# Router logits as one accumulated product in 16 columns, both halves of attention together, and a recurrence step moved into an expert product

## The chip, the cores and the metric

The kernel runs on 1 core of one Trainium2 chip. The time is that of one execution on the device in microseconds (us), the median of several runs. TensorE (PE) multiplies, VectorE (DVE), ScalarE (ACT) and GpSimd (POOL) do the elementwise work, SyncE (SP) issues most transfers. PEld is TensorE's loading of weights, which can run beside its matmuls.

## The reference, cut to what matters

```
x = x + attn_a(layernorm(x))         # gated linear attention, then a GELU feed-forward inside
x = x + ffn(layernorm(x))            # mixture of experts
x = x + attn_b(layernorm(x))         # recurrence h = tanh(x_t B + h A^T), then C and W_out
x = x + ffn(layernorm(x))            # the same mixture of experts again

def ffn(x):                          # per token, 8 experts, 2 chosen
    logits = x @ router_w.T          # (tokens, 8)
    probs = softmax(logits)
    topk_vals, topk_idx = top_k(probs, 2)
    topk_w = topk_vals / (topk_vals.sum(-1) + 1e-6)
    out = ((x @ expert[topk_idx] + probs[topk_idx]) * topk_w).sum(over the two)
```

x has 8 batches of 1024 tokens of 256 values, all float32. The recurrence goes over the 1024 positions of a batch, one after another.

## The kernel before

The 1024 positions are cut into 32 rounds of 32 positions; with 8 batches a round has 256 tokens (`TOK`), held as 2 tiles (`TILES`) of 128 tokens. A round passes through 8 stages (the `live(it, n)` of each engine's `body`), and the stages of 8 different rounds are interleaved in one iteration of the loop: stage 1 and 2 are the linear attention, 3 its output and the feed-forward, 4 the first router and its experts (`m1`), 5 the 32 steps of the recurrence, 6 its end and the second router (`m2`), 7 the second experts. The first 8 iterations and the last 7 are written out, 24 run as a loop. All stages that this document speaks of (attention of stage 2, first experts of stage 4, the recurrence of stage 5, the second router of stage 6) run together in iterations 6 to 33, which are 28; each stage runs 32 times.

Each engine has its own order of instructions, written out by hand in its `body`, and waits on semaphores by count. There is no scheduler.

Products in full precision are made in three single-pass float32r matmuls for each chunk of 128 (`product`, L1247 to L1255: lead x lead, lead x rest, rest x lead). The left operand of each is split in a lead (`yT[:, 0]`, a copy by ScalarE) and a rest (`yT[:, 1]`, a subtraction by VectorE). An expert product (`moe`, out of `we` and `yT`) has six such matmuls of 512 columns for a pair of experts and a tile of tokens; there are 8 (`G1_0` to `G1_7`) for each router.

The recurrence has one small matmul for each step (`step`, L1271, 8 columns). ScalarE makes two tanh of it (`state_of`, L566 and L567), VectorE the split into parts that are exact in float32r (`split_state`, L858), and only then can TensorE issue the next step. The hand-written orders put one or more other products between two steps.

The router: TensorE transposes the normalised tokens (L1260), ScalarE and VectorE split them (`yT`), and `logits` (L1285) makes four float32 matmuls with `rw`, 32 stationary columns of which 8 hold the router's weights: one for each part and chunk, each in its own strip of 32 columns of the array and so in its own 32 output partitions. ScalarE copies the result into `m.y[:, 0]` (L696 for the first router, L734 for the second), `logits_by_token` (L1292) transposes it back in two 128x128 transposes, and VectorE adds the four pieces (`top_two`, L898) and picks the two experts.

Attention: `attend(i, ...)` (L1331) makes 16 matmuls for tile i, in strips of 32 columns. `attend(0)` stood ahead of step 14, `attend(1)` behind step 14 and the second router's logits. ScalarE squares the result (`osq`, L731) once both are done.

Of the kernel before, what the change touches and what calls it, by code (L numbers as in the profile page):

```python
# [39 lines left out]
ROUTED = 32  # L40
# [56 lines left out]
def build(nc, x, wts, out):  # L97
    ctx = ExitStack()
    with ctx:
# [35 lines left out]
        rw = sb("rw", [P, KC, ROUTED])  # L135
# [98 lines left out]
        late_sync = [(raw(W_1, KC * FF), wts["W1"]), (rw[:, :, 0:E], wts["router_w"]), (b1[:], wts["b1"])]  # L234
# [147 lines left out]
        def _(pool):  # L382
# [6 lines left out]
            g.memset(rw[:], 0.0)  # L389
# [143 lines left out]
        def _(act):  # L533
# [13 lines left out]
            def split_late():  # L547
                act.wait_ge(sem("weights_psum"), 2)
                act.wait_ge(sem("a_loaded"), A_LOADED)
                act.wait_ge(sem("late"), LATE)  # L550
                a.activation(a_lead, a_raw, ACT.Copy)
                a.activation(cw[ROW_LEAD:ROW_LEAD + 1, :], bout[ROW_LEAD:ROW_LEAD + 1, :], ACT.Copy)
                a.activation(bout_lead, bout[ROW_REST:ROW_REST + 1, :], ACT.Copy)
                a.activation(cw_lead, ps[0:NB, BANK["RB"], 0:D], ACT.Copy).then_inc(sem("weights_lead"), 1)
                act.wait_ge(sem("weights_rest"), REST["scaled_out"])
                a.activation(wa[:, 0, W_O:W_END], raw(W_O, W_END - W_O), ACT.Copy).then_inc(sem("weights_lead"), 1)
# [63 lines left out]
            def body(it):  # L620
# [73 lines left out]
                if live(it, 5):  # L694
                    act.wait_ge(sem("LT1"), c5)
                    a.activation(m1.y[:, 0, :], ps[:, BANK["L1"], 0:TOK], ACT.Copy).then_inc(sem("lT1"), 1)  # L696
# [35 lines left out]
                if live(it, 7):  # L732
                    act.wait_ge(sem("LT2"), c7)
                    a.activation(m2.y[:, 0, :], ps[:, BANK["L2"], 0:TOK], ACT.Copy).then_inc(sem("lT2"), 1)  # L734
# [88 lines left out]
        def _(dve):  # L823
# [15 lines left out]
            def split_late():  # L839
                dve.wait_ge(sem("weights_lead"), LEAD["late"])  # L840
                v.tensor_tensor(wa[:, 1, W_O:W_END], raw(W_O, W_END - W_O), wa[:, 0, W_O:W_END].bitcast(F32), ALU.subtract).then_inc(sem("weights_rest"), 1)
# [53 lines left out]
            def top_two(m, bank, count):  # L895

                pieces = ps[:, bank, TOK:2 * TOK].rearrange("p (i s w) -> p i s w", i=TILES, w=ROUTED)[:, :, :, 0:E]
                v.tensor_reduce(m.lg, pieces.rearrange("p i s e -> p i e s"), AX.X, ALU.add).then_inc(sem(f"lg{m.s}"), 1)  # L898
                target = value(dve, count)
                dve.wait_ge(sem("pads_zero"), 1)  # L900
                dve.wait_ge(sem(f"lg{m.s}"), target)
                for i in range(TILES):
                    ins = v.max(m.mx[:, i, :], m.lg[:, i, :])
                ins.then_inc(sem(f"mx{m.s}"), 1)
# [326 lines left out]
        def _(pe):  # L1231
# [15 lines left out]
            def product(dst, left, right, chunks):  # L1247


                n = 0  # L1250
                for c in range(chunks):
                    for lp, rp in ((0, 0), (0, 1), (1, 0)):
                        n += 1
                        ins = t.matmul(dst, left(lp, c), right(rp, c), start=(n == 1), stop=(n == 3 * chunks))  # L1254
                return ins  # L1255
# [7 lines left out]
            def moe(m, k, bank):  # L1263

                i, pr = k // PAIRS, k % PAIRS
                right = lambda p, c: we[:, p, c * E * D + pr * 2 * D:c * E * D + (pr + 1) * 2 * D]
                return product(ps[:, bank, :], lambda p, c: m.yT[:, p, c, i * P:(i + 1) * P], right, KC)
# [12 lines left out]
            def logits(m, bank):  # L1280

                for part in range(2):
                    for c in range(KC):
                        g = part * KC + c
                        ins = t.matmul(ps[ROUTED * g:ROUTED * (g + 1), bank, 0:TOK], rw[:, c, :], m.yT[:, part, c, :].bitcast(F32),  # L1285
                                       start=True, stop=True, skip_group_check=True)
                return ins

            def logits_by_token(m, bank):

                for i in range(TILES):
                    ins = t.transpose(ps[:, bank, TOK + i * P:TOK + (i + 1) * P], m.y[:, 0, i * P:(i + 1) * P], ident)  # L1292
                return ins
# [42 lines left out]
            def body(it):  # L1336
# [201 lines left out]
                if live(it, 4):  # L1538
# [6 lines left out]
                    pe.wait_ge(sem("lT1"), c4)  # L1545
# [26 lines left out]
                if live(it, 2):  # L1572
# [3 lines left out]
                    attend(0, isinstance(it, int) and it == 2)  # L1576
                if live(it, 5):
                    step(14, c5)
# [5 lines left out]
                if live(it, 2):  # L1584
                    attend(1, False).then_inc(sem("O11"), 1)
                if live(it, 5):
                    step(15, c5)
                if live(it, 4):
                    for name, count in readers(it, "G1_4"):
                        pe.wait_ge(sem(name), count)  # L1590
                    moe(m1, 4, BANK["G1_4"]).then_inc(sem("moe1"), 1)
                if live(it, 5):
                    step(16, c5)
                if live(it, 6):
                    pe.wait_ge(sem("lT2"), c6)
                    logits_by_token(m2, BANK["L2"]).then_inc(sem("L2"), 1)
# [76 lines left out]
```

## Time and profile before

| | before |
|---|---|
| runs | 1694.19 us median of 3 (1693.38 to 1694.59) |
| span of the profiled execution | 1692.7 us |
| time of the profiled execution beside its span | none given apart from the span |
| PE busy | 1591.6 us (94%) |
| PEld busy | 1324.5 us (78%) |
| DVE busy | 1274.3 us (75%) |
| ACT busy | 1051.2 us (62%) |
| POOL busy | 823.1 us (49%) |
| mean granted TensorE clock | 0.974 |

The span is from the first to the last instruction of one execution. Busy is the time in which an engine has at least one instruction in work; matmuls are pipelined and overlap, so the distance between the starts of two instructions says more than how long one is. The granted clock is 1.00 in the stretches used below, which is 2.4 GHz.

### The profile page before, as it was taken

How to read it: one execution, taken by the hardware profiler on the slowest of the kernel's cores; microseconds unless marked ns; L12 is line 12 of the kernel's file. 1: busy time of each engine (PE TensorE's matmuls, PEld its weight loads, DVE VectorE, ACT ScalarE, POOL GpSimd, SP SyncE). 2: the span in 40 equal slices, each digit the busy share in tenths (PEclk: the TensorE clock that was granted, in tenths of full speed). 3: DMA queues.
4: the chain of work that ended last, by engine and by line, in shares of the span. 5: the costliest groups of instructions: out<-in, count | busy, mean ns of one | idle time of the engine just before them, and what ended most of it. 6: DMA issues, size and time to landing. Idle time of an engine off the chain costs nothing.

```text
span 1692.7 us, 51627 instructions
## 1 busy us (share of the span) xinstructions
PE 1591.6 (94%) x16840; PEld 1324.5 (78%) x16840; DVE 1274.3 (75%) x4556; ACT 1051.2 (62%) x3851; POOL 823.1 (49%) x1294
## 2 busy tenths in 40 slices
PE   4588999999999999999999999999999999998866
PEld 3477888888888888888888888888888888887654
DVE  4566777887788778787888787887888877876544
ACT  4656666666766666666666666666666667655431
POOL 3554454554555455545454554454545545543211
PEclk7799999999999999999999999999999999999978
DMA  5211111111111111011111111111111111110000
GB/s 151 84 57 45 52 58 58 42 39 43 43 56 56 56 51 43 31 52 47 56 56 56 46 42 35 50 50 56 56 56 43 37 44 44 52 52 8 7 7 13
DMA packets 117250, 81.49 MB, mean 48 GB/s; under 512 B 42016, under 2 KB 108224, under 8 KB 117056
## 3 DMA queue, kind: packets, MB, share of 16 engines
q1 hardware_dynamic: 116208, 80.10, 15.4%
q8 instruction: 38, 0.62, 0.2%
q10 hardware_dynamic: 976, 0.54, 0.1%
q14 instruction: 28, 0.23, 0.0%
HBM read 47.06 MB, written 33.55 MB: 48 GB/s over the span
## 4 chain that ended last, share of the span: by engine, by line
PE 82%; DVE 6%; issue 3%; DMA 3%; ACT 2%; SPq 2%; POOL 1%; ACTq 0%; DVEq 0%; POOLq 0%
PE ps L1254 62%; PE ps L1260 4%; PE ps L1271 4%; PE ps L1285 2%; PE ps L1301 2%; PE ps L1442 2%; PE ps L1331 2%; DMA xag<-in_x 2%; PE ps L1321 2%; PE ps L1312 1%; DVE hs L858 1%; DVE att L947 1%; DVE dstate L1075 1%; PE ps L1292 1%; DMA arow<-att 1%
## 5 line engine op out<-in xcount | busy, mean ns | idle before, releaser
L1254 PE MATMUL ps<-we,yT 128*128 128x512 f32 x3072 | 824.5, 411 | 0.3 <-DVE h2Ts L953 0.3
L1254 PEld LDWEIGHTS ps<-we,yT 128*128 128x128 f32 x3072 | 546.5, 191 | 100.9 <-issue 1.1
L566 ACT ACTIVATE h_lead<-ps 48x8 fp32r<-48x8 f32 x1024 | 172.4, 168 | 443.8 <-PE ps L1271 430.3
L858 DVE SCALAR_TENSOR_TENSOR hs<-ps,cst,h_lead 48x8 fp32r<-48x8 f32 x1024 | 224.7, 219 | 223.8 <-ACT ps L567 216.1
L1271 PEld LDWEIGHTS ps<-hs,aT 128*128 128x128 f32 x1024 | 195.1, 191 | 126.4 <-DVE hs L858 99.1
L1271 PE MATMUL ps<-hs,aT 128*128 128x8 f32 x1024 | 215.9, 211 | 39.7 <-DVE hs L858 38.3
L890 DVE SCALAR_TENSOR_TENSOR stage<-ps,coef,stage 128x256 f32<-128x256 f32 x384 | 183.1, 477 | 13.8 <-POOL stage L433 5.0
L890 DVE SCALAR_TENSOR_TENSOR acc<-ps,coef,acc 128x256 f32<-128x256 f32 x384 | 181.7, 473 | 6.6 <-POOL acc L433 2.7
L518 POOL TENSOR_TENSOR orstd<-omean,mhalf 128x32 f32<-128x32 f32 x32 | 174.6, 5455 | 0.2
L567 ACT ACTIVATE ps<-ps 48x8 f32<-48x8 f32 x1024 | 162.8, 159 | 0.0
L431 POOL TENSOR_TENSOR part<-part 128x256 f32<-128x256 f32 x64 | 46.9, 732 | 204.2 <-ACT part L584 201.8
L431 POOL TENSOR_TENSOR stage<-stage 128x256 f32<-128x256 f32 x64 | 47.8, 746 | 187.7 <-ACT stage L584 187.7
L1254 PE MATMUL ps<-h2Ts,wa 128*128 128x256 f32 x768 | 106.9, 289 | 3.7 <-DVE h2Ts L953 3.7
L1254 PE MATMUL ps<-wa,gTs 128*128 128x256 f32 x768 | 108.1, 291 | 0.7 <-DVE gTs L953 0.6
L1254 PE MATMUL ps<-wa,hTs 128*128 128x512 f32 x384 | 103.3, 406 | 0.0
L1254 PEld LDWEIGHTS ps<-wa,gTs 128*128 128x128 f32 x768 | 96.0, 191 | 7.0 <-issue 6.0
L1254 PEld LDWEIGHTS ps<-h2Ts,wa 128*128 128x128 f32 x768 | 95.8, 191 | 5.4 <-DVE h2Ts L953 3.9
L512 POOL TENSOR_SCALAR omean<-oss 128x32 f32<-128x32 f32 x32 | 8.9, 277 | 178.5 <-DVE oss L1172 178.5
L575 ACT ACTIVATE ps<-ps,lnb,lnw 128x256 f32<-128x256 f32 x128 | 67.2, 529 | 30.5 <-PE ps L1260 30.5
L1254 PEld LDWEIGHTS ps<-wa,hTs 128*128 128x128 f32 x384 | 67.6, 188 | 14.1
L401 POOL TENSOR_SCALAR ra<-mv_a 128x2 f32<-128x2 f32 x32 | 6.1, 191 | 145.0 <-DVE mv_a L877 145.0
L606 ACT ACTIVATE qx<-qt,cst 128x256 f32<-128x256 f32 x128 | 64.4, 505 | 1.4 <-DVE qt L977 1.4
(184 smaller groups left out, 3200.4 us busy)
## 6 DMA issues: line engine op xcount, KB each, us to landing
arow<-att SPq DMA_DIRECT2D x32, 512.0 KB, 2.8
atx<-arow SPq DMA_DIRECT2D x128, 128.0 KB, 2.8
vrow<-vtok SPq DMA_DIRECT2D x32, 256.0 KB, 2.1
vx<-vrow SPq DMA_DIRECT2D x128, 64.0 KB, 2.0
out<-stage SPq DMA_DIRECT2D x64, 128.0 KB
xin<-in_x SPq DMA_DIRECT2D x62, 128.0 KB
xag<-in_x SPq DMA_DIRECT2D x62, 128.0 KB
stage<-in_experts SPq DMA_DIRECT2D x1, 2048.0 KB, 9.5
```

The lines of the kernel that those rows point to most:

```text
L431: g.tensor_tensor(m.part[:, i, 0, :], m.part[:, i, 0, :], m.part[:, i, 1, :], ALU.add).then_inc(sem(f"part{m.s}"), 1)
L518: g.tensor_tensor(orstd[:], omean[:], mhalf[:], ALU.pow).then_inc(sem("orstd"), 1)
L566: a.activation(h_lead[:], ps[0:NB, BANK["RB"], k * B:(k + 1) * B], ACT.Tanh)
L567: a.activation(h_whole, ps[0:NB, BANK["RB"], k * B:(k + 1) * B], ACT.Tanh).then_inc(sem("rnn_tanh"), 1)
L575: a.activation(ps[:, bank, c * TOK:(c + 1) * TOK], ps[:, bank, c * TOK:(c + 1) * TOK], ACT.Identity, bias=lnb[:, c:c + 1], scale=lnw[:, c: ...
L606: return a.activation(qx[:, h, :, :], bt(qt[:]), ACT.Identity, scale=headmask[:, h:h + 1])
L858: v.scalar_tensor_tensor(hs[0:NB, :, k], h_whole, keeps_rest, h_lead[:].bitcast(F32), ALU.mult, ALU.subtract).then_inc(sem("rnn_h"), 1)
L890: v.scalar_tensor_tensor(m.acc[:, i, :], ps[:, bank, half * D:(half + 1) * D], m.coef[:, i, e:e + 1], m.acc[:, i, :], ALU.mult, ALU.add).t ...
L1254: ins = t.matmul(dst, left(lp, c), right(rp, c), start=(n == 1), stop=(n == 3 * chunks))
L1260: ins = t.transpose(ps[:, dst_bank, c * TOK + i * P:c * TOK + (i + 1) * P], src[:, i, c * P:(c + 1) * P], ident)
L1271: return t.matmul(ps[0:NP, BANK["RB"], k * B:(k + 1) * B], aT[:], hs[:, :, (k - 1) % TS], start=False, stop=True, skip_group_check=True)
L1285: ins = t.matmul(ps[ROUTED * g:ROUTED * (g + 1), bank, 0:TOK], rw[:, c, :], m.yT[:, part, c, :].bitcast(F32), start=True, stop=True, skip_ ...
```

## The change

The router's weights are split as the others are, into a lead and a rest of 8 columns each, in one array `rws` of 16 columns (`ROUTED = 2 * E`). `logits` makes four float32r matmuls, one for each part and chunk of the tokens, that all add up in the same 16 output partitions. ScalarE copies 16 partitions instead of 128. `logits_by_token` transposes 16 partitions: its stationary operand has 16 rows and 128 columns, its moving one 16 columns. `top_two` adds two pieces instead of four. The wait ahead of `logits_by_token` becomes a wait of its own, with another on `pads_zero` ahead of it.

In TensorE's order `attend(1)` moves directly behind `attend(0)`, ahead of step 14. The fifth expert product of the first router (`G1_4`) starts behind the second router's logits with two of its six matmuls, then comes step 15, then the other four.

```diff
-ROUTED = 32
+ROUTED = 2 * E
...
-        rw = sb("rw", [P, KC, ROUTED])
+        rw, rws = sb("rw", [P, KC, E]), sb("rws", [P, KC, ROUTED], F32R)
...
-            g.memset(rw[:], 0.0)
...
+                a.activation(rws[:, :, 0:E], rw[:], ACT.Copy)
...
-                    a.activation(m1.y[:, 0, :], ps[:, BANK["L1"], 0:TOK], ACT.Copy).then_inc(sem("lT1"), 1)
+                    a.activation(m1.y[0:ROUTED, 0, :], ps[0:ROUTED, BANK["L1"], 0:TOK], ACT.Copy).then_inc(sem("lT1"), 1)
...
+                v.tensor_tensor(rws[:, :, E:ROUTED], rw[:], rws[:, :, 0:E].bitcast(F32), ALU.subtract)
...
-                pieces = ps[:, bank, TOK:2 * TOK].rearrange("p (i s w) -> p i s w", i=TILES, w=ROUTED)[:, :, :, 0:E]
-                v.tensor_reduce(m.lg, pieces.rearrange("p i s e -> p i e s"), AX.X, ALU.add).then_inc(sem(f"lg{m.s}"), 1)
+                pieces = ps[:, bank, TOK:TOK + TILES * ROUTED].rearrange("p (i s e) -> p i e s", i=TILES, e=E)
+                v.tensor_reduce(m.lg, pieces, AX.X, ALU.add).then_inc(sem(f"lg{m.s}"), 1)
...
-            def product(dst, left, right, chunks):
-
-
-                n = 0
-                for c in range(chunks):
-                    for lp, rp in ((0, 0), (0, 1), (1, 0)):
-                        n += 1
-                        ins = t.matmul(dst, left(lp, c), right(rp, c), start=(n == 1), stop=(n == 3 * chunks))
+            def product(dst, left, right, chunks, begin=0, end=None):
+
+                terms = [(c, lp, rp) for c in range(chunks) for lp, rp in ((0, 0), (0, 1), (1, 0))]
+                for n, (c, lp, rp) in list(enumerate(terms))[begin:end]:
+                    ins = t.matmul(dst, left(lp, c), right(rp, c), start=(n == 0), stop=(n == 3 * chunks - 1))
                 return ins
...
             def logits(m, bank):
 
+                n = 0
                 for part in range(2):
                     for c in range(KC):
-                        g = part * KC + c
-                        ins = t.matmul(ps[ROUTED * g:ROUTED * (g + 1), bank, 0:TOK], rw[:, c, :], m.yT[:, part, c, :].bitcast(F32),
-                                       start=True, stop=True, skip_group_check=True)
+                        n += 1
+                        ins = t.matmul(ps[0:ROUTED, bank, 0:TOK], rws[:, c, :], m.yT[:, part, c, :], start=(n == 1), stop=(n == 2 * KC))
                 return ins
 
             def logits_by_token(m, bank):
 
                 for i in range(TILES):
-                    ins = t.transpose(ps[:, bank, TOK + i * P:TOK + (i + 1) * P], m.y[:, 0, i * P:(i + 1) * P], ident)
+                    ins = t.transpose(ps[:, bank, TOK + i * ROUTED:TOK + (i + 1) * ROUTED], m.y[0:ROUTED, 0, i * P:(i + 1) * P], ident[0:ROUTED, 0:ROUTED])
                 return ins
...
                     attend(0, isinstance(it, int) and it == 2)
+                if live(it, 2):
+                    attend(1, False).then_inc(sem("O11"), 1)
                 if live(it, 5):
                     step(14, c5)
...
                     logits(m2, BANK["L2"]).then_inc(sem("LT2"), 1)
-                if live(it, 2):
-                    attend(1, False).then_inc(sem("O11"), 1)
+                if live(it, 4):
+                    for name, count in readers(it, "G1_4"):
+                        pe.wait_ge(sem(name), count)
+                    moe(m1, 4, BANK["G1_4"], 0, 2)
                 if live(it, 5):
                     step(15, c5)
                 if live(it, 4):
-                    for name, count in readers(it, "G1_4"):
-                        pe.wait_ge(sem(name), count)
-                    moe(m1, 4, BANK["G1_4"]).then_inc(sem("moe1"), 1)
+                    moe(m1, 4, BANK["G1_4"], 2).then_inc(sem("moe1"), 1)
```

On TensorE, in the loop, from the attention of stage 2 to the second router's transposes, before (L1331 is `attend`, L1271 a recurrence step, here 14, 15 and 16, L1285 `logits`, L1254 with `we` an expert product, L1292 `logits_by_token`):

```order
L1331 MATMUL ps<-vx,atx 32x64 x16
L1277 REGISTER_ALU
L1271 MATMUL ps<-hs,aT 128x8
L1285 MATMUL ps<-yT,rw 32x256 x4
L1331 MATMUL ps<-vx,atx 32x64 x16
L1277 REGISTER_ALU
L1271 MATMUL ps<-hs,aT 128x8
L1254 MATMUL ps<-we,yT 128x512 x6
L1277 REGISTER_ALU
L1271 MATMUL ps<-hs,aT 128x8
L1292 MATMUL ps<-cst,stage 128x128 x2
```

The same place in the changed kernel, whose lines are L1329, L1269, L1284, L1252 and L1290:

```order
L1329 MATMUL ps<-vx,atx 32x64 x32
L1275 REGISTER_ALU
L1269 MATMUL ps<-hs,aT 128x8
L1284 MATMUL ps<-yT,rws 16x256 x4
L1252 MATMUL ps<-we,yT 128x512 x2
L1275 REGISTER_ALU
L1269 MATMUL ps<-hs,aT 128x8
L1252 MATMUL ps<-we,yT 128x512 x4
L1275 REGISTER_ALU
L1269 MATMUL ps<-hs,aT 128x8
L1290 MATMUL ps<-cst,stage 128x16 x2
```

The 32 attention matmuls stand together ahead of step 14, and step 15 stands behind the second of the six expert matmuls. The number of matmuls and steps is the same.

The first router on TensorE, before, from the last transposes of tokens (L1260) over steps 9 and 10:

```order
L1260 MATMUL ps<-cst,stage 128x128 x4
L1285 MATMUL ps<-yT,rw 32x256 x4
L1277 REGISTER_ALU
L1271 MATMUL ps<-hs,aT 128x8
L1254 MATMUL ps<-we,yT 128x512 x6
L1292 MATMUL ps<-cst,ym 128x128 x2
L1277 REGISTER_ALU
L1271 MATMUL ps<-hs,aT 128x8
```

And in the changed kernel:

```order
L1258 MATMUL ps<-cst,stage 128x128 x4
L1284 MATMUL ps<-yT,rws 16x256 x4
L1275 REGISTER_ALU
L1269 MATMUL ps<-hs,aT 128x8
L1252 MATMUL ps<-we,yT 128x512 x6
L1290 MATMUL ps<-cst,ym 128x16 x2
L1275 REGISTER_ALU
L1269 MATMUL ps<-hs,aT 128x8
```

Here nothing moves; the outputs of the logits go from 32 partitions in four strips to 16, and each transpose gives 16 columns instead of 128.

## Rows read from the trace of the kernel before

**Rows 1.** The page: the span.

```profile
span 1692.7 us, 51627 instructions
```

**Rows 2.** Busy time of one round: stretch, length, then each engine's busy time.

```profile
851.00:899.63 48.63, 48.40 (x527) 40.59 (x526) 39.27 (x142) 32.38 (x121) 25.51 (x41) 1.00 0.16 49
```

**Rows 3.** Order in time, TensorE, around scores: start, length, what, tile, count.

```profile
859.52 0.17 PE L1271 MATMUL ps<-hs,aT 128*128 128x8 f32 x1
859.62 0.50 PE L1301 MATMUL ps<-qx,kt 32*32 32x128 f32 x32
860.05 0.98 PE L1254 MATMUL ps<-wa,oTs 128*128 128x256 f32 x6
```

**Rows 4.** Order in time, TensorE's weight loads; in brackets idle before it.

```profile
860.05 0.77 PEld L1254 LDWEIGHTS ps<-wa,oTs 128*128 128x128 f32 x6 [0.20 <-issue]
...
878.71 0.20 PEld L1292 LDWEIGHTS ps<-cst,stage 128*128 128x128 f32 x2
```

**Rows 5.** Order in time, TensorE, at the first router, steps 9 and 10.

```profile
867.49 0.64 PE L1285 MATMUL ps<-yT,rw 128*32 128x256 f32 x8
868.10 0.27 PE L1271 MATMUL ps<-hs,aT 128*128 128x8 f32 x1
868.23 1.65 PE L1254 MATMUL ps<-we,yT 128*128 128x512 f32 x6
869.72 0.38 PE L1292 MATMUL ps<-cst,ym 128*128 128x128 f32 x2
869.85 0.25 PE L1271 MATMUL ps<-hs,aT 128*128 128x8 f32 x1
869.97 1.64 PE L1254 MATMUL ps<-we,yT 128*128 128x512 f32 x6
```

**Rows 6.** Order in time, TensorE, attention to second router, steps 14 to 17.

```profile
875.29 0.65 PE L1331 MATMUL ps<-vx,atx 128*32 128x64 f32 x32
875.87 0.27 PE L1271 MATMUL ps<-hs,aT 128*128 128x8 f32 x1
876.08 0.64 PE L1285 MATMUL ps<-yT,rw 128*32 128x256 f32 x8
876.53 0.63 PE L1331 MATMUL ps<-vx,atx 128*32 128x64 f32 x32
877.09 0.27 PE L1271 MATMUL ps<-hs,aT 128*128 128x8 f32 x1
877.22 1.65 PE L1254 MATMUL ps<-we,yT 128*128 128x512 f32 x6
878.71 0.17 PE L1271 MATMUL ps<-hs,aT 128*128 128x8 f32 x1
878.74 0.41 PE L1292 MATMUL ps<-cst,stage 128*128 128x128 f32 x2
878.91 0.96 PE L1254 MATMUL ps<-hTs,wz 128*128 128x256 f32 x6
879.70 0.17 PE L1271 MATMUL ps<-hs,aT 128*128 128x8 f32 x1
```

**Rows 7.** Order in time, ScalarE, tanh of steps 15 and 16 and between.

```profile
877.40 0.17 ACT L566 ACTIVATE h_lead<-ps 48x8 fp32r<-48x8 f32 x1
...
877.53 0.62 ACT L731 ACTIVATE osq<-ps 128x512 f32<-128x512 f32 x1
878.05 0.36 ACT L734 ACTIVATE stage<-ps 128x256 f32<-128x256 f32 x1
878.94 0.17 ACT L566 ACTIVATE h_lead<-ps 48x8 fp32r<-48x8 f32 x1 [0.53 <-PE ps L1271]
```

**Rows 8.** Order in time, VectorE, from split 15 to split 16.

```profile
877.67 0.23 DVE L858 SCALAR_TENSOR_TENSOR hs<-ps,cst,h_lead 48x8 fp32r<-48x8 f32 x1
...
878.84 0.47 DVE L890 SCALAR_TENSOR_TENSOR acc<-ps,coef,acc 128x256 f32<-128x256 f32 x1
879.23 0.22 DVE L858 SCALAR_TENSOR_TENSOR hs<-ps,cst,h_lead 48x8 fp32r<-48x8 f32 x1
```

More of the change, by code:

```diff
@@ L233, in build @@
                         (b2g[:], wts["gk_b2"])]
-        late_sync = [(raw(W_1, KC * FF), wts["W1"]), (rw[:, :, 0:E], wts["router_w"]), (b1[:], wts["b1"])]
+        late_sync = [(raw(W_1, KC * FF), wts["W1"]), (rw[:], wts["router_w"]), (b1[:], wts["b1"])]
         late_sync += [(cT[:, :, n * N:(n + 1) * N], wts["C"]) for n in range(3)]
@@ L733, in body @@
                     act.wait_ge(sem("LT2"), c7)
-                    a.activation(m2.y[:, 0, :], ps[:, BANK["L2"], 0:TOK], ACT.Copy).then_inc(sem("lT2"), 1)
+                    a.activation(m2.y[0:ROUTED, 0, :], ps[0:ROUTED, BANK["L2"], 0:TOK], ACT.Copy).then_inc(sem("lT2"), 1)
                 if live(it, 6):
@@ L1261, in transposed, with moe @@
                 return ins
-            def moe(m, k, bank):
+            def moe(m, k, bank, begin=0, end=None):
                 i, pr = k // PAIRS, k % PAIRS
                 right = lambda p, c: we[:, p, c * E * D + pr * 2 * D:c * E * D + (pr + 1) * 2 * D]
-                return product(ps[:, bank, :], lambda p, c: m.yT[:, p, c, i * P:(i + 1) * P], right, KC)
+                return product(ps[:, bank, :], lambda p, c: m.yT[:, p, c, i * P:(i + 1) * P], right, KC, begin, end)
             def recur(k):
@@ L1544, in body @@
                     moe(m1, 0, BANK["G1_0"]).then_inc(sem("moe1"), 1)
-                    pe.wait_ge(sem("lT1"), c4)
+                    target = value(pe, c4)
+                    pe.wait_ge(sem("pads_zero"), 1)
+                    pe.wait_ge(sem("lT1"), target)
                     logits_by_token(m1, BANK["L1"]).then_inc(sem("L1"), 1)
@@ L1594, in body @@
                 if live(it, 6):
-                    pe.wait_ge(sem("lT2"), c6)
+                    target = value(pe, c6)
+                    pe.wait_ge(sem("pads_zero"), 1)
+                    pe.wait_ge(sem("lT2"), target)
                     logits_by_token(m2, BANK["L2"]).then_inc(sem("L2"), 1)
```

## The prediction

> **What bounds the kernel now.** I read the page first, then the busy table of one round in the middle, then the order in time of TensorE, ScalarE and VectorE around the code that the change touches. The page gives the span, 1692.7 us [rows 1]; the page's execution has no other time of its own, and the three runs have a median of 1694.19, so what lies around a span is 1.5 us, which I add at the end. The busy table [rows 2] covers exactly one round of the loop: 48.63 us, of which TensorE is busy 48.40, VectorE 39.27, ScalarE 32.38. TensorE is the bound with almost nothing idle. So a change counts by what it does to the times at which TensorE's instructions start, 32 times, and I price everything as distance between starts. The one other thing that can hold TensorE is the recurrence: step k+1 needs VectorE's split of step k, which needs ScalarE's two tanh. As long as these come back in time they cost nothing.
>
> **Reading the price of a switch.** The matmuls have shapes of rows*columns used in the array. Products are 128*128, the attention's small ones 32*32 or 128*32. Between equal shapes a product starts 0.03 after the recurrence step ahead of it (878.71 to 878.74 [rows 6]). From a step to the 32*32 scores it is 0.10 [rows 3]: entering another shape costs 0.07. Leaving: the last weight load of the scores ends at 859.85 and the product's first comes 0.20 later, with the engine's load side idle [rows 4]; the last score matmul has 128 columns, which take 0.11 (the two 128-column transposes and the step behind them: 869.72 to 869.85 is 0.13 with 0.02 for the step [rows 5]), so leaving costs 0.09 beyond the stream. In addition the next step's own weights are loaded late, and what follows it starts 0.13 behind it instead of 0.03 (868.10 to 868.23 [rows 5], 877.09 to 877.22 [rows 6]).
>
> The Trainium skill (TensorEngine Tiling (Array Packing), section Key Properties) says that changing the tiling mode, not only the tile, drains TensorE. The trace agrees for 32*32 and 128*32 with the 0.07 and 0.09 above; no row shows it for 16 columns or 16 rows in the middle of a stream.
>
> **1. Router logits (both routers).** Before: four float32 matmuls side by side in four 32-column strips, two passes each (x8), together 0.61 from the first start to the next step [rows 5]. Now: four single-pass matmuls of 256 columns into the same 16 output partitions, one after another. A 256-column product matmul in the stream takes 0.12 to 0.13 (six in 0.79 [rows 6]). Four are 0.48 to 0.52, and leaving 0.09 to 0.10: 0.57 to 0.62, I take 0.58, because 16 columns of weights are a short load. Gain 0.03. The title says the whole array, but the matmul uses 16 of 128 columns, and I take it to be as foreign a shape as 32 columns were: entries and exits stay.
>
> **2. Logits by token, first router.** Two transposes of 128x128 become two with 128 stationary columns on 16 rows and only 16 moving columns. The shape was 128*128, as its neighbours; now it is 16*128, so it is entered and left. Before, first transpose to next product: 0.25 (869.72 to 869.97 [rows 5]). Now: 0.07 later in; the second transpose 0.07 behind the first (two weight loads of 0.14 fit in 0.20, so they start 0.06 apart [rows 4]; that load still has 128 columns, and 16 moving columns hide nothing of it); 0.15 to the next start (0.09 to leave, 0.06 for the last load, which nothing covers); 0.13 from the step to the product. That is 0.42, so +0.17. The first load is exposed too, by up to 0.06: +0.17 to +0.23, I take +0.18.
>
> The Trainium skill (TensorE: Matmul & The Clock Gate, section LDWEIGHTS) says a weight load takes columns divided by 1.2 GHz whatever the number of rows, an estimate of 0.107 for these 128 columns. By that the two loads of a place would cost 0.21 instead of 0.12, 5.8 us more over 64 places. It speaks against the change as the rows do.
>
> **3. Attention halves together, step 15 inside the expert product.** The same matmuls, steps and switches in another order, so what matters is where steps 14 to 17 land. Before [rows 6]: step 14 at 875.87, 15 at 877.09, 16 at 878.71, 17 at 879.70. Now, from the first half's start at 875.29: the first half without its exit 0.46 (0.56 less 0.10), the second 0.56, step 14 at 876.31 (+0.44). Logits 0.21 behind it (as now), 876.52; product at 877.10. Six expert matmuls take 1.49, 0.23 each after the first two, so the first two take 0.57: step 15 at 877.67 (+0.58). Then 0.03, 0.55 and two of 0.23: step 16 at 878.71, the same time as before. TensorE by itself gains nothing.
>
> But the two engines behind it do not keep up. **ScalarE:** the tanh of step 15 starts at 877.90 (0.23 behind its step, as for step 16), then the square of the attention output 0.13 later, then the copy of the second router's logits 0.52 after that, 0.36 long: the distances of [rows 7]. It ends at 878.91 instead of 878.41. The transposes that read it want to start at 878.81; they start at about 878.96, so a wait of 0.15 is new, and it now lies as a wait of its own ahead of them. Behind it: 0.07, 0.15, and 0.79 to 0.81 for the gate product: step 17 at 879.98. **VectorE:** split 15 runs 0.27 behind the tanh, so at 878.17 instead of 877.67; between it and split 16 stand the normalised input half, the rest of h2 and a combine, without a gap, 1.56 from split to split [rows 8]. Split 16 then starts at 879.73, ends 0.22 later, and step 17 can't start before 880.00. Both chains give the same: step 17 is 0.29 later than 879.70. Behind step 17 the stream is packed as before (steps are 1.5 apart) and nothing in front of it gives the time back.
>
> The second router's transposes alone, without these chains, would cost +0.14 (0.10 + 0.07 + 0.15 + 0.81 = 1.13 against 878.71 to 879.70, 0.99). This is inside the 0.29, and counts only in the 4 rounds of the second router in which not all four stages run. All of them run in 28 rounds.
>
> **4. The rest.** One small ScalarE copy and one VectorE subtraction of 16 columns once at the start, a memset less, a shorter reduction of the logits on VectorE, and a separate wait in front of the first router's transposes. The copy that this wait asks for (0.36 for the second router's [rows 7]) lies under an expert product of 1.49 [rows 5]. All 0; if the product did not cover it, it would be 0.1 a round, 3 us.
>
> **Sum.** 28 x 0.29 = 8.1; 4 x 0.14 = 0.6; 32 x 0.18 = 5.8; 32 x -0.03 = -1.0. Together +13.5: span 1706.2, time 1707.7, say 1707.5. Bounds of the terms: exits at 0.09 or 0.13 and loads hidden or not give 0.17 to 0.23 and -0.04 to +0.01, the chain 0.20 to 0.35: +10 to +18, so 1704 to 1712.
>
> **Rivals.**
> *The 16-row transposes cost no switch.* For it: no row shows that shape. Against: both other small shapes pay. Then the first router gains 0.10 (two matmuls of 0.06 instead of 0.11), but step 17 is still held by VectorE at 880.00: 28 x 0.29 - 32 x 0.10 - 32 x 0.03 - 4 x 0.10 = +3.5: 1697.7. Chance 0.17.
> *Faster: 16 columns do count as the whole array, for logits and transposes.* Then the logits take 0.50 instead of 0.61 and what follows starts 0.03 instead of 0.13 behind its step; with the transposes the first router gains 0.31, 9.9 us in all. At the second router step 15 comes early, but ScalarE's work ahead of its tanh (877.40 [rows 7]) moves with step 14 by 0.44, so split 16 comes 0.44 late and step 17 about 0.24: +6.7; the 4 rounds without attention give 1.6. Net -4.8: 1689.4. It decides as soon as a router block saves more than 0.3. Chance 0.15.
> *Serial matmuls in one strip of 16 columns don't hide their loads.* For it: side by side each strip had its own. Against: the attention changes weights in every strip at each of its matmuls and two halves still take 0.45 to 0.58. It would add 0.07 three times, at 64 places: 13 us more, 1721. Chance 0.10.
> *My forecast*: chance 0.58.
>
> **Numbers.** Runs of this kernel differ by 0.07%; I take 0.2% (3.4 us) as what a measurement can tell. Faster by more: the second rival, 0.16 with some rest. Within: most of the first rival, 0.13. Slower: 0.71. The range of 8 in 10 takes in the first rival, half of the second and stops short of the third: 1689 to 1717; that of the likeliest case alone is 1704 to 1712.
>
> **What the profile after would show.** Step to 16-row transposes 0.10, not 0.03, and 0.13 behind the next step: the switch is there. Logits to next start 0.58. Step 15 to 17 about 2.3 us instead of 2.6, step 14 to 17 3.67 instead of 3.83, and a wait of the second transposes on ScalarE's logits copy, or of step 17 on VectorE: 28 to 31 times. A round of 49.05 to 49.1 instead of 48.63. I am wrong if the round is at or under 48.63, which would mean that the small shapes start like their neighbours, or that ScalarE and VectorE find room that I don't see.

## The result and the profile after

The changed kernel takes 1702.12 us (median of 16 runs, 1698.07 to 1706.85), the kernel before 1694.97 in the 16 runs beside it (1690.40 to 1700.72). The ratio is 1.0032, with a 95% interval of 1.0021 to 1.0042: slower by 3.6 to 7.1 us, with 5.4 at the ratio itself; the two medians lie 7.2 us apart, at the upper end of that. The forecast was 1707.5, 0.8% more than before. The sign is right and the time lies in the wide range, but under the 1704 to 1712 of the likeliest case. By the ratio the loss is less than half of what was forecast, and it comes from one of the two places that were named, the stretch up to step 17. The other, the first router, adds nothing to a round.

The page of the changed kernel, its span and the busy time of the whole span:

```profile
span 1698.9 us, 51180 instructions
...
PE 1590.5 (94%) x16584; PEld 1330.1 (78%) x16584; DVE 1268.3 (75%) x4557; ACT 1045.1 (62%) x3852; POOL 823.3 (48%) x1293
```

The span is 6.2 us longer than in [rows 1]. The busy table over one round, which answers to [rows 2]:

```profile
857.69:906.56 48.87, 48.32 (x520) 40.72 (x519) 38.99 (x142) 32.13 (x120) 25.52 (x41) 1.00 0.16 48
```

The round is 0.24 us longer, with TensorE *less* busy by 0.08: it is idle for 0.55 us of it, before for 0.23. Over 28 full rounds 0.25 (the difference of the medians below) gives 7.0 us, at the upper end of what the runs show. The table of waits names the one that is new, first of the two rows (engine, what waits, for whom, us in total, times, the longest). In the kernel before it came once, with 0.5 us:

```profile
PE ps L1290 <- ACT stage L734: 9.5, 29, 0.6
...
PE ps L1269 <- DVE hs L859: 38.1, 80, 1.3
```

The second router's transposes wait for ScalarE's copy of the logits, 29 times, 0.33 each. Next the order in time of TensorE at the two places, answering to [rows 5] and [rows 6]:

```profile
872.99 0.64 PE L1284 MATMUL ps<-yT,rws 128*16 128x256 f32 x4
873.60 0.27 PE L1269 MATMUL ps<-hs,aT 128*128 128x8 f32 x1
873.73 1.65 PE L1252 MATMUL ps<-we,yT 128*128 128x512 f32 x6
875.31 0.29 PE L1290 MATMUL ps<-cst,ym 16*128 16x16 f32 x2
875.53 0.27 PE L1269 MATMUL ps<-hs,aT 128*128 128x8 f32 x1
875.67 1.66 PE L1252 MATMUL ps<-we,yT 128*128 128x512 f32 x6
877.16 0.17 PE L1269 MATMUL ps<-hs,aT 128*128 128x8 f32 x1
...
880.77 1.10 PE L1329 MATMUL ps<-vx,atx 128*32 128x64 f32 x64
881.80 0.27 PE L1269 MATMUL ps<-hs,aT 128*128 128x8 f32 x1
881.94 0.63 PE L1284 MATMUL ps<-yT,rws 128*16 128x256 f32 x4
882.40 0.62 PE L1252 MATMUL ps<-we,yT 128*128 128x512 f32 x2
882.86 0.17 PE L1269 MATMUL ps<-hs,aT 128*128 128x8 f32 x1
882.89 1.16 PE L1252 MATMUL ps<-we,yT 128*128 128x512 f32 x4
883.88 0.21 PE L1269 MATMUL ps<-hs,aT 128*128 128x8 f32 x1
884.41 0.26 PE L1290 MATMUL ps<-cst,stage 16*128 16x16 f32 x2 [0.32 <-ACT stage L734]
884.60 0.98 PE L1252 MATMUL ps<-hTs,wz 128*128 128x256 f32 x6
885.42 0.17 PE L1269 MATMUL ps<-hs,aT 128*128 128x8 f32 x1
```

At the first router the transposes start 1.58 behind their product's start instead of 1.49, and the next product 0.36 behind them instead of 0.25: step 9 to step 10 is 1.93 where it was 1.75. At the second router the attention's start to step 17 is 4.65 where [rows 6] give 4.41: +0.24. ScalarE over the same stretch:

```profile
883.29 0.16 ACT L566 ACTIVATE h_lead<-ps 48x8 fp32r<-48x8 f32 x1
883.34 0.16 ACT L567 ACTIVATE ps<-ps 48x8 f32<-48x8 f32 x1
883.40 0.62 ACT L731 ACTIVATE osq<-ps 128x512 f32<-128x512 f32 x1
883.92 0.35 ACT L734 ACTIVATE stage<-ps 16x256 f32<-16x256 f32 x1
```

The copy starts 0.04 behind step 16 and ends 0.39 behind it; before it started 0.66 ahead of step 16 [rows 6, 7]. It handles 16 partitions instead of 128 and is no shorter (0.35, 0.36).

One round says where TensorE is held, not what the rounds have in common. So I took for every kernel the median distance from one recurrence step to the next over rounds 3 to 26 (worked out from the starts in the traces). The steps that are not listed agree within 0.02 between before and after, and within 0.04 over all kernels.

```
step k to k+1   9    10   11   12   13   14   15   16   17   18   round
before        1.75 1.66 1.61 1.57 1.18 1.22 1.61 0.99 1.51 1.51  48.62
after         1.93 1.61 1.51 1.52 1.62 1.06 1.02 1.53 1.51 1.51  48.87
order only    1.75 1.67 1.61 1.57 1.62 1.34 1.04 1.22 1.55 1.50  48.89
router only   1.93 1.61 1.51 1.52 1.18 1.28 1.61 1.14 1.51 1.51  48.84
wide transp.  1.75 1.63 1.62 1.58 1.62 1.06 1.02 1.49 1.51 1.51  48.83
copy first    1.93 1.61 1.51 1.52 1.62 1.06 1.02 1.38 1.61 1.51  48.83
split 16      1.93 1.61 1.50 1.53 1.62 1.06 1.03 1.17 1.51 1.72  48.74
  and wide    1.75 1.64 1.62 1.58 1.62 1.06 1.04 1.04 1.56 1.81  48.73
  and 10, 11  1.75 1.59 1.51 1.51 1.62 1.06 1.02 1.06 1.57 1.81  48.54
all           1.75 1.59 1.51 1.51 1.62 1.06 1.05 1.04 1.55 1.51  48.21
all, old ord. 1.74 1.59 1.51 1.51 1.18 1.27 1.61 0.99 1.51 1.51  48.47
before twice  1.97 1.59 1.50 1.54 1.18 1.22 1.61 0.99 1.51 1.51  48.62
before 10, 11 1.75 1.59 1.50 1.51 1.17 1.22 1.61 1.04 1.61 1.50  48.52
32 columns    1.95 1.62 1.51 1.51 1.62 1.06 1.04 1.53 1.51 1.51  48.86
```

Steps 9 to 13: 6.59 before, 6.57 after. Steps 13 to 17: 5.00 before, 5.23 after. The first router's loss of 0.18 is given back by steps 10, 11 and 12, which got shorter by 0.05, 0.10 and 0.05. All of the round's loss stands between steps 13 and 17.

What gave it back stands in the trace of before, in the weight loads of TensorE, a view that the prediction read only elsewhere (in brackets: idle ahead, and for whom):

```profile
869.83 0.19 PEld L1271 LDWEIGHTS ps<-hs,aT 128*128 128x128 f32 x1
869.94 1.23 PEld L1254 LDWEIGHTS ps<-we,yT 128*128 128x128 f32 x6
871.51 0.19 PEld L1271 LDWEIGHTS ps<-hs,aT 128*128 128x128 f32 x1 [0.34 <-DVE hs L858]
871.62 1.23 PEld L1254 LDWEIGHTS ps<-we,yT 128*128 128x128 f32 x6
873.09 0.19 PEld L1271 LDWEIGHTS ps<-hs,aT 128*128 128x128 f32 x1 [0.24 <-DVE hs L858]
```

Steps 11 and 12 were already waiting for VectorE's splits, in each of the 24 rounds of the table, 0.34 and 0.24 in the median. The matmul rows don't show it, since six matmuls of 1.65 cover the gap in them; the load rows do, and so does the distance between steps, 1.66 and 1.61 where a packed stretch of the same content takes 1.51.

### The profile page after: what moved, and what is told of

It is laid out like the page before. It is cut to its first block, busy times and chain, and to the rows that moved or that the text cites. A ratio compares the mean times of both kernels' runs of the same rounds, so it can differ in the third digit from the quotient of the medians.

```text
span 1698.9 us, 51180 instructions
## 1 busy us (share of the span) xinstructions
PE 1590.5 (94%) x16584; PEld 1330.1 (78%) x16584; DVE 1268.3 (75%) x4557; ACT 1045.1 (62%) x3852; POOL 823.3 (48%) x1293
## 4 chain that ended last, share of the span: by engine, by line
PE 79%; DVE 6%; ACT 5%; issue 4%; DMA 2%; SPq 1%; POOL 1%; ACTq 0%; DVEq 0%; POOLq 0%
PE ps L1252 61%; PE ps L1258 4%; PE ps L1269 3%; PE ps L1299 2%; PE ps L1329 2%; PE ps L1440 2%; PE ps L1319 2%; PE ps L1310 2%; DVE hs L859 1%; DMA xag<-in_x 1%; PE ps L1284 1%; DVE att L948 1%; DVE dstate L1076 1%; ACT ps L575 1%; PE ps L1290 1%
## 5 line engine op out<-in xcount | busy, mean ns | idle before, releaser
L1252 PE MATMUL ps<-we,yT 128*128 128x512 f32 x3072 | 816.9, 409 | 1.1 <-DVE h2Ts L954 1.1
L1252 PEld LDWEIGHTS ps<-we,yT 128*128 128x128 f32 x3072 | 540.8, 190 | 98.4 <-DVE h2Ts L954 1.3
L1269 PEld LDWEIGHTS ps<-hs,aT 128*128 128x128 f32 x1024 | 195.4, 191 | 115.1 <-DVE hs L859 85.1
L1269 PE MATMUL ps<-hs,aT 128*128 128x8 f32 x1024 | 209.3, 204 | 38.5 <-DVE hs L859 38.1
L1252 PE MATMUL ps<-h2Ts,wa 128*128 128x256 f32 x768 | 108.6, 292 | 3.6 <-DVE h2Ts L954 3.6
L1252 PE MATMUL ps<-wa,gTs 128*128 128x256 f32 x768 | 106.4, 288 | 0.7 <-DVE gTs L954 0.6
L1252 PE MATMUL ps<-wa,hTs 128*128 128x512 f32 x384 | 105.8, 413 | 0.0
L1252 PEld LDWEIGHTS ps<-h2Ts,wa 128*128 128x128 f32 x768 | 97.2, 193 | 5.6 <-DVE h2Ts L954 3.9
L1252 PEld LDWEIGHTS ps<-wa,gTs 128*128 128x128 f32 x768 | 94.3, 188 | 7.0 <-issue 6.0
L575 ACT ACTIVATE ps<-ps,lnb,lnw 128x256 f32<-128x256 f32 x128 | 67.2, 528 | 30.6 <-PE ps L1258 30.6
L1252 PEld LDWEIGHTS ps<-wa,hTs 128*128 128x128 f32 x384 | 69.2, 193 | 14.1
L610 ACT ACTIVATE gT<-ps,b 128x256 f32<-128x256 f32 x128 | 59.1, 465 | 8.9 <-PE ps L1252 8.5
```

The costliest lines, as they stand in the source:

```text
L575: a.activation(ps[:, bank, c * TOK:(c + 1) * TOK], ps[:, bank, c * TOK:(c + 1) * TOK], ACT.Identity, bias=lnb[:, c:c + 1], scale=lnw[:, c: ...
L610: return a.activation(gT[:, f, :], ps[:, BANK["F1A" if f < 2 else "F1B"], f % 2 * TOK:(f % 2 + 1) * TOK], ACT.Gelu, bias=b1[:, f:f + 1])
L1252: ins = t.matmul(dst, left(lp, c), right(rp, c), start=(n == 0), stop=(n == 3 * chunks - 1))
L1269: return t.matmul(ps[0:NP, BANK["RB"], k * B:(k + 1) * B], aT[:], hs[:, :, (k - 1) % TS], start=False, stop=True, skip_group_check=True)
```

## The experiments

Each ratio is to the kernel before, run beside it, with its 95% interval; a round is the median of the table above. 'Packed' is a distance of 1.51, the shortest between steps around six products.

**1. The new order alone**, with the old router.

```diff
     attend(0, ...)
+    attend(1, False).then_inc(sem("O11"), 1)
     step(14, c5)
...
+    moe(m1, 4, BANK["G1_4"], 0, 2)
     step(15, c5)
+    moe(m1, 4, BANK["G1_4"], 2)
```

> The kernel before with the new order on TensorE alone (both halves of attention together, step 15 behind the second of six expert matmuls); the router is the old one, in four strips of 32 columns. Theory A (the loss comes from steps 14 to 17, where ScalarE's copy of the second router's logits comes late behind the later step 15): a round in the middle of 48.80 to 48.95 us instead of 48.63, time +0.3 to +0.6%. Theory B (the loss is the new shape of the router's transposes, the order is free): a round of 48.63, time unchanged.

1.0046 (1.0023 to 1.0069), a round of 48.89, +0.27. The load row of the transposes in this kernel, which are 128 wide here:

```profile
735.43 0.20 PEld L1289 LDWEIGHTS ps<-cst,stage 128*128 128x128 f32 x2 [0.27 <-ACT stage L734]
```

The same wait, without any narrow transpose near it. So the order alone makes ScalarE's copy late, as theory A has it. In TensorE's own work the order gains nothing here: 13 to 16 is 4.00, before 4.01. The loss is 16 to 17 (+0.23) and what follows it (+0.04).

**2. The new router alone**, in the old order.

> The changed kernel with the old order of attention, steps 14 and 15 and the fifth expert product; so the new router alone. Theory A (what the first router's narrow transposes cost is taken back at steps 10 to 13, where VectorE held TensorE anyway; 16-column logits start like a whole-array matmul): step 9 to step 13 as before, 6.59 us, a round of 48.60 to 48.70. Theory B (as forecast: each narrow transpose place counts, 0.15 at the first router and 0.14 at the second): a round of 48.85 to 48.95.

1.0026 (1.0003 to 1.0049), a round of 48.84, +0.22. 9 to 13 went as theory A has it: 9 to 10 is +0.18, and all of it is back by step 13. The total is at the lower edge of theory B all the same, by two other places. 16 to 17 is +0.15 for the switch in and out of the second router's transposes, where the forecast had 0.14; theory A had left that out. And 14 to 15 is 0.06 longer. The losses of the two parts, 0.27 and 0.22, don't add up: together 0.25. In both together the copy's wait of 0.3 is there anyway, and the narrow transposes add only 0.04 behind it (16 to 17 is 1.53 in the changed kernel and 1.49 in experiment 3).

What the new logits cost depends on what stands beside them. These are medians over the same 24 rounds, from the first start of the logits to the start of what follows:

```
                     then the attention     then an expert product
logits before        0.46 (before)          0.57 (order only)
logits in 16 columns 0.56 (router only)     0.47 (after)
```

From step 14 to the logits it is 0.20 with the old ones and 0.13 with the new. So the new logits start and end like a whole-array product and pay 0.10 where they border on the attention's strips; the old ones are the other way round. The two parts of the change need each other: the new order is what puts the new logits between whole-array work.

**3. The transposes 128 wide again**, in the changed kernel. `top_two` reads the 16 of 128 columns that hold something.

```diff
-    ins = t.transpose(ps[:, bank, TOK + i * ROUTED:TOK + (i + 1) * ROUTED], m.y[0:ROUTED, 0, i * P:(i + 1) * P], ident[0:ROUTED, 0:ROUTED])
+    ins = t.transpose(ps[:, bank, TOK + i * P:TOK + (i + 1) * P], m.y[:, 0, i * P:(i + 1) * P], ident)
```

> The changed kernel with the two transposes of the logits back to 128 rows and 128 columns (16 of the 128 output columns are used); logits stay in 16 columns, order as changed. Theory A (transposes at the first router are covered by VectorE's hold, at the second by the wait for ScalarE's copy): the place at the first router is 0.2 us shorter on TensorE, but a round stays at 48.82 to 48.87. Theory B (the shape switch is on the path): 48.55 to 48.60.

1.0033 (1.0015 to 1.0050), a round of 48.83. 9 to 10 falls by 0.18 and 10 to 13 takes back 0.19. The loads of steps 11 and 12 there:

```profile
724.72 0.19 PEld L1269 LDWEIGHTS ps<-hs,aT 128*128 128x128 f32 x1 [0.31 <-DVE hs L859]
...
726.30 0.19 PEld L1269 LDWEIGHTS ps<-hs,aT 128*128 128x128 f32 x1 [0.24 <-DVE hs L859]
```

VectorE's waits are there again with nearly the lengths of before. The switch at the first router is real and costs a round nothing, as theory A has it.

**4. The logits copy ahead of the square**, in the changed kernel, on ScalarE.

```diff
+    act.wait_ge(sem("LT2"), c7)
+    a.activation(m2.y[0:ROUTED, 0, :], ...)
     act.wait_ge(sem("O11"), c3)
     a.activation(osq[:], ..., ACT.Square)
```

> The changed kernel, where ScalarE copies the second router's logits ahead of the square of the attention output instead of behind it. Theory A (this copy is what step 17 waits for, and VectorE's split 16 is the next to hold it, 0.14 us earlier): the wait on ScalarE at the narrow transposes is gone, step 13 to 17 is 5.09 us instead of 5.23, a round of 48.72 to 48.76. Theory B (VectorE's chain alone holds step 17, as the second sum of the prediction had it): a round stays at 48.87.

1.0017 (0.9998 to 1.0036), a round of 48.83; theory A had 48.72 to 48.76. Steps 13 to 17 fall to 5.08 from 5.23, as it had, but 17 to 18 rises to 1.61 and takes most of that back. The loads of step 17 and behind it:

```profile
733.90 0.19 PEld L1269 LDWEIGHTS ps<-hs,aT 128*128 128x128 f32 x1 [0.25 <-DVE hs L859]
734.00 0.99 PEld L1252 LDWEIGHTS ps<-we,yT 128*128 128x128 f32 x5
```

Where the copy no longer holds the transposes, VectorE's split 16 holds step 17, 0.15 earlier than the copy did. The prediction had both chains end together. And a step that came late has its load in the open: the product's first load starts 0.10 behind the step's (734.00, 733.90), so the product starts 0.13 behind the step instead of 0.03.

**5. VectorE's split 16 ahead of the combine as well.**

```diff
+    split_state(16, c5)
     combine(m1, 2, 0, BANK["G1_2"], c4)
-    split_state(16, c5)
```

> The changed kernel with ScalarE's copy of the second router's logits first, and VectorE's split of step 16 ahead of the combine of expert product 2 instead of behind it. Theory A (with the copy first, step 17 is held by VectorE's split 16, and a step that TensorE has waited for costs another 0.10 us behind it, because its weights and the next ones are loaded in the open): step 16 to 17 falls from 1.38 to 1.12 to 1.16, 17 to 18 from 1.61 to 1.51, a round of 48.48 to 48.55, faster than the kernel before by 0.2%. Theory B (the place is bound by TensorE and what one step gains the next loses): a round stays at 48.83.

1.0015 (1.0004 to 1.0027), a round of 48.74; both theories missed, A with 48.48 to 48.55 and B with 48.83. 13 to 17 is 4.88, under the 5.00 of before, and 17 to 18 is packed. But 18 to 19 is 1.72. The load behind step 18, and two of VectorE's rows, of which it waited for the second:

```profile
736.30 0.76 PEld L1252 LDWEIGHTS ps<-we,yT 128*128 128x128 f32 x4 [0.27 <-DVE sub L914]
```

```profile
735.14 0.18 DVE L899 TENSOR_REDUCE lm<-ps 128x16 f32<-128x32 f32 x1
...
736.09 0.16 DVE L914 TENSOR_TENSOR sub<-lm 128x20 f32<-128x20 f32 x1
```

The second router's choice of experts on VectorE, which waits for those logits and stands behind both combines, is now late for the expert product that takes the same PSUM bank (`G1_6` and `L2` are both bank 0). TensorE ran ahead into the next wait of the same engine. The rows show more: of the choice only the sum, L899, reads the bank, and it is done at 735.32, while the kernel's table of readers (`BANK_ORDER`) has TensorE wait for L914 (`sub2`), which reads `lm` and ends at 736.25. What a wait on L899 alone would give was not run.

**6 and 7.** The fifth with transposes 128 wide, and then with splits 10 and 11 moved ahead of the first router's choice and its denominators.

```diff
+    split_state(10, c5)
     top_two(m1, BANK["L1"], c4)
-    split_state(10, c5)
...
     below_top(m1, c4)
+    split_state(11, c5)
     dve.wait_ge(sem("p1"), c4)
     denominators(m1, c4)
-    split_state(11, c5)
```

> As the run with split 16 early, and the transposes of the logits on 128 rows and columns as before the change. Theory A (the shape switch of the 16-row transposes now is on the path at the second router, 0.10 to 0.15, and at the first it is still covered by VectorE): step 9 to 13 stays at 6.58, step 16 to 17 about 1.00, a round of 48.35 to 48.42. Theory B (the switch is on the path at both): 48.15 to 48.20. If it is covered at both: 48.50.

> As the run before it, and VectorE's split of step 10 ahead of the first router's top two, its split of step 11 ahead of the denominators. Theory A (steps 11 and 12 wait for VectorE, which does router work ahead of their splits, and that is what hid the first router's extra TensorE time): step 9 to 13 falls from 6.58 to 6.25 to 6.35, a round about 0.25 to 0.33 under the run before it, 48.05 to 48.15. Theory B (these distances are TensorE's own work): no change against the run before it.

The sixth: 1.0018 (1.0007 to 1.0029) with a round of 48.73. It took 0.13 off 16 to 17, and 17 to 19 ate it. The seventh: 0.9989 (0.9976 to 1.0002) with 48.54. It shortened 9 to 13 from 6.59 to 6.36, where 6.25 to 6.35 was expected, and the round fell by 0.19. Both rounds miss what was expected (48.35 to 48.42 and 48.05 to 48.15), by 0.30 or more; 0.30 of that is the wait at 18 to 19 (1.81 instead of 1.51).

**8. More work for TensorE in the kernel before**: the first router's transposes twice.

> The kernel before, where TensorE makes the first router's two 128x128 transposes of the logits twice: 0.22 us more of its work in each round at that place. Theory A (VectorE's hold of steps 11 and 12 takes it in): step 9 to 10 is 1.97 instead of 1.75, but step 9 to 13 stays within 6.59 to 6.65, a round of 48.62 to 48.68, time within 0.1%. Theory B (TensorE is the bound there, the reading behind the forecast): a round of 48.84, +0.4%.

The place in this kernel, TensorE:

```profile
729.22 0.27 PE L1271 MATMUL ps<-hs,aT 128*128 128x8 f32 x1
729.35 1.64 PE L1254 MATMUL ps<-we,yT 128*128 128x512 f32 x6
730.83 0.60 PE L1292 MATMUL ps<-cst,ym 128*128 128x128 f32 x4
731.18 0.25 PE L1271 MATMUL ps<-hs,aT 128*128 128x8 f32 x1
731.29 1.64 PE L1254 MATMUL ps<-we,yT 128*128 128x512 f32 x6
732.77 0.17 PE L1271 MATMUL ps<-hs,aT 128*128 128x8 f32 x1
```

The median of 9 to 10 is 1.97, +0.22, and the round is 48.62 as before: that place has 0.2 of slack, whatever fills it. The time, though, is 1.0023 (1.0012 to 1.0034), 4 us that the middle rounds don't show; theory A had within 0.1%, theory B +0.4%. In its trace the fourth round begins 5.6 us later than in that of before (276.2, 270.6). But over the traces of all fourteen kernels it begins at 268.3 to 276.8 with no relation to the edits, and the first rounds wait for transfers (6.0 us for `w2g` before, 7.0 here), so one trace of each does not tell what there is due to the edit. This stays open.

**9. 32 columns instead of 16**, in the changed kernel, still in one strip.

```diff
-ROUTED = 2 * E
+ROUTED = 4 * E
```

> The changed kernel, but with 32 stationary columns instead of 16 in the router's accumulated product (the last 16 are zero), 32 output partitions and 32-row transposes. Theory A (what makes the old router expensive to enter and leave is that its matmuls stand in four strips at once; a product in the first strip alone starts and ends like a whole-array one, whatever its width): step to logits 0.13, last logits matmul to expert product 0.12 as with 16 columns. Theory B (32 columns are the array's narrow shape, 16 are not): 0.20 and 0.35. Round 48.87 by A, 49.0 or more by B.

A single run, 1702.09, so its time says nothing; its trace has a round of 48.86. The logits, TensorE:

```profile
731.76 0.27 PE L1270 MATMUL ps<-hs,aT 128*128 128x8 f32 x1
731.89 0.64 PE L1285 MATMUL ps<-yT,rws 128*32 128x256 f32 x4
732.36 0.62 PE L1253 MATMUL ps<-we,yT 128*128 128x512 f32 x2
```

0.13 into the logits and 0.47 to the product, as with 16 columns (0.14, 0.46). So 32 columns cost what 16 do, and the number of columns is not what made the old logits dear; four strips side by side, or the two passes of float32, are left. These two were not told apart: the attention, beside which the old logits pay nothing (experiment 2), has both as well.

**10. All of it, and the combines moved out of the way**: the seventh, with the second router's choice directly behind split 16 and the combines behind it.

```diff
     split_state(16, c5)
+    top_two(m2, BANK["L2"], c6)
     combine(m1, 2, 0, BANK["G1_2"], c4)
-    combine(m1, 2, 1, BANK["G1_2"], c4)
-    top_two(m2, BANK["L2"], c6)
...
     v.tensor_reduce(oss[:], osq[:], AX.X, ALU.add)
+    combine(m1, 2, 1, BANK["G1_2"], c4)
```

> As the run with splits 10 and 11 early, and VectorE's second-router top two moved directly behind split 16, ahead of the two combines of expert product 2, the second of which goes behind the reduction of the squares. Theory A (step 18 to 19 takes 1.81 there because the expert product between them waits for VectorE to have read the second router's logits): 18 to 19 falls to 1.50 to 1.55, a round of 48.22 to 48.30, time 0.6 to 0.8% under the kernel before. Theory B (VectorE has no room, the wait moves to a later step): a round of 48.45 to 48.55.

0.9942 (0.9920 to 0.9965), 1684.42 us, a round of 48.21. TensorE from step 14 on:

```profile
724.00 0.27 PE L1270 MATMUL ps<-hs,aT 128*128 128x8 f32 x1
724.13 0.63 PE L1285 MATMUL ps<-yT,rws 128*16 128x256 f32 x4
724.60 0.62 PE L1253 MATMUL ps<-we,yT 128*128 128x512 f32 x2
725.06 0.17 PE L1270 MATMUL ps<-hs,aT 128*128 128x8 f32 x1
725.09 1.18 PE L1253 MATMUL ps<-we,yT 128*128 128x512 f32 x4
726.11 0.18 PE L1270 MATMUL ps<-hs,aT 128*128 128x8 f32 x1
726.15 0.44 PE L1291 MATMUL ps<-cst,stage 128*128 128x128 f32 x2
726.34 0.95 PE L1253 MATMUL ps<-hTs,wz 128*128 128x256 f32 x6
727.12 0.22 PE L1270 MATMUL ps<-hs,aT 128*128 128x8 f32 x1
```

Step 14 to 17 is 3.12 here, against 3.62 in the changed kernel, and none of these rows carries a wait. The round is just under the 48.22 to 48.30 of theory A, the fall of the time by 0.58% just short of its 0.6 to 0.8%; 18 to 19 is 1.51 as expected.

**11. The tenth in the old TensorE order.**

> The same kernel with the old order of attention, steps 14 and 15 and the fifth expert product on TensorE. Theory A (the new order is worth 0.2 us a round once ScalarE and VectorE no longer hold step 17): a round of 48.42 to 48.50. Theory B (the order is worth nothing to TensorE, which has the same work in it): as with the new order, 48.22 to 48.30.

0.9958 (0.9941 to 0.9976), a round of 48.47. In the medians the new order is worth 0.26 a round here: 13 to 17 is 5.05 without it, 4.77 with it. The intervals of the two ratios overlap, so this rests on the traces. With the same new router but VectorE and ScalarE in their old orders, it cost 0.03 (48.87 in the changed kernel, 48.84 in experiment 2), although 13 to 16 on TensorE was 0.37 shorter with it (3.70, 4.07). The 0.27 that it cost in experiment 1 is no fair comparison, since that has the old router, with which the order shortens nothing on TensorE. Whether it would gain there with the other engines' new orders was not run.

**12. The kernel before, with splits 10 and 11 moved.**

> The kernel before, with VectorE's split 10 ahead of the first router's top two and split 11 ahead of the denominators, and nothing else. Theory A (VectorE held TensorE at steps 10 to 13 before the change already, by 0.2 us a round): step 9 to 13 is 6.36 to 6.40 instead of 6.59, a round of 48.39 to 48.43, time -0.3 to -0.5%. Theory B (TensorE was the bound there): unchanged.

0.9983 (0.9966 to 1.0000), a round of 48.52. 9 to 13 falls by 0.24 to 6.35, and the loads of steps 11 and 12 wait in none of the 24 rounds: TensorE had been held there in the kernel before. 0.15 comes back at 16 to 18, where the load of step 17 now waits for VectorE in 10 of the 24 rounds (before in 2), so the round misses the expected 48.39 to 48.43.

## Why the prediction was right in sign and wrong in size

**What bounds the kernel now** is the step that failed: "TensorE is the bound with almost nothing idle. So a change counts by what it does to the times at which TensorE's instructions start, 32 times". The 48.40 of 48.63 that TensorE is busy were read as work. They held waits: 9 to 13 took 6.59 where 6.35 is enough (experiment 12). So a start that moves is not a round that moves. The recurrence was named as "the one other thing that can hold TensorE", but it was followed behind steps 15 and 16 alone, and not behind steps 10 and 11, where it did.

**2. Logits by token, first router** had the right size at its place: forecast +0.18, measured +0.18 from step 9 to 10 (0.09 in, 0.22 to the step, 0.14 to the product). Entered as +0.18 x 32 = 5.8 us, it was worth nothing in a round: VectorE held steps 11 and 12 by more than that before (0.24). That is shown for the middle rounds from both sides, by taking it away (3) and by putting as much in (8), with the open 4 us of experiment 8 beside it. It is by far the largest part of the error: without it the sum is +7.7 instead of +13.5, beside +5.4 by the runs' ratio and +6.2 by the spans, of which 4.1 stand ahead of the fourth round, whose start varies that much between traces.

**1. Router logits.** Forecast 0.58 and a gain of 0.03. The matmuls start 0.13 to 0.14 behind their step and the product 0.12 behind the last of them: 0.46 at the second router, no price for a switch. "I take it to be as foreign a shape as 32 columns were" is what was wrong in this term. The gain of 0.03 did not come at the first router: there the logits' start to step 9 is 0.61 as before, since split 8 holds step 9 (its load waits 0.26 for VectorE) and the start is set by the tokens.

**3. Attention halves together** was right as a mechanism and 0.06 too large: 0.29 forecast, 0.23 measured. Step 14 to 15 was forecast at 1.36 and is 1.06, by the cheaper logits (0.19) and by the first two expert matmuls (0.46, not 0.57). So "TensorE by itself gains nothing" is wrong: 13 to 16 is 3.70 instead of 4.01, where no change was forecast. That gained nothing in time, because ScalarE is still busy with the work of step 14 (L575 and L726) when step 15 is done: its tanh starts 0.43 behind the step, where 0.23 was taken, though [rows 6, 7] already have 0.31 for this step. This is what the second rival said of step 15, and its price, 0.24, is nearest to the measured one. ScalarE's copy ends 3.50 behind the attention's start, where 3.62 was forecast, and it sets step 17; that is why the total came out near although step 16 did not. The wait for the copy is the one named, 29 times where 28 to 31 were forecast, but 0.33 long instead of 0.15, and step 15 to 17 is 2.56 instead of 2.3. The chain on VectorE, said to end at the same time, ends 0.15 before it (4): it had split 15 at 1.86 behind step 14, which is 1.74, and took a distance of 1.56 from there to split 16 that is 1.45 here.

**The rivals.** "The 16-row transposes cost no switch" is false: they pay on both sides at both routers. "16 columns do count as the whole array" is true of the logits and false of the transposes, which have 16 rows. "Serial matmuls in one strip don't hide their loads" is false.

The Trainium skill (TensorEngine Tiling (Array Packing), section Key Properties) has a change of mode drain TensorE. The trace agrees for 16 rows (0.09 in, 0.14 behind the next step). For 128 rows with 16 or 32 columns in one strip it shows no such price beside whole-array products; the 16 columns pay 0.10 beside the attention's strips (experiment 2). By another page of the Trainium skill (TensorE: Matmul & The Clock Gate, section LDWEIGHTS), two loads of 128 columns would take an estimated 0.21. Here the two of the transposes take 0.20 from the first start to the last end and start about 0.06 apart, in float32, while a load of float32r is followed by the next 0.11 later. What the place cost more was 0.18 from step to step, as the rows had it, so the further 5.8 us that this rule threatened did not come.

**What stays open:** the 4 us of experiment 8 that lie outside the middle rounds, and so how much of the measured loss of the others lies there; also which of strips and passes costs the old logits their way in and out beside whole-array work.

## What to carry to other kernels

An engine that reads 99% busy (48.32 to 48.40 of a round here) can still be waiting: before pricing a shift, compare each distance between marks with the shortest one of the same content, and read the idle time of the load rows, not that of the matmul rows. A cost that is smaller than the wait behind it is free, and a gain made just ahead of a wait is worth nothing; both must be followed to the next wait of the same late engine, and only the distance over all of them counts. An order that shortens one engine's own work can be worth nothing until the engines behind it are put in the same order: with the new router, the new order cost 0.03 a round at first and gained 0.26 once VectorE and ScalarE served the recurrence first.

## What the hardware showed beyond that

- A small matmul that TensorE had to wait for costs 0.08 to 0.10 more behind it (0.11 to 0.13 instead of 0.03 to the next product): its own load and the next one stand in the open, 0.10 apart. It is seen at step 17 in experiment 4, and at step 9, whose load waits for VectorE, both before and after.
- A float32r product of 16 or 32 columns and 128 rows, in one strip, starts and ends beside products of 128 columns as these do (0.13 behind an exposed step, 0.12 from its last matmul to the product). A transpose of 16 rows does not (0.09 in, 0.14 behind the next step).
- A ScalarE copy of 16 partitions takes as long as one of 128 (0.35 and 0.36 at the second router, 0.40 both times at the first).
